# Second layer norm of a GNN kernel: last tile's product in column halves, batch statistics, final scaling shared by VectorE and ScalarE

## The reference

```python
def _L1_gnn_ref(x, edge_index, W1, b1, W2, b2):
    h = jax.nn.relu(x @ W1 + b1) @ W2 + b2
    row, col = (edge_index[0], edge_index[1])
    agg = jax.ops.segment_sum(h[col], row, num_segments=h.shape[0])
    return h + agg

def _layernorm(x, axis=-1, eps=1e-05):
    m = jnp.mean(x, axis=axis, keepdims=True)
    v = jnp.var(x, axis=axis, keepdims=True)
    return (x - m) / jnp.sqrt(v + eps)

x = _layernorm(x + _L1_gnn_ref(x, edge_index, W1, b1, W2, b2), axis=-1)
```

## Time and profile before

| what | value |
|---|---|
| runs | 252.47, 253.5, 253.42 us, median 253.42 |
| the profiled execution's own time | 252.69 us |
| its span | 250.7 us |
| TensorE's granted clock, mean | 0.974 |
| busy: TensorE, VectorE, ScalarE, GpSimd | 92%, 62%, 53%, 35% of the span |
| last matmul ends | about 245.03 us |
| last store issued, landed | 248.0, about 250.25 us |

### The profile page before, as it was taken

How to read it: one execution, slowest core, us unless ns; L and a number is a source line. 1 busy time by engine, 2 the same in 40 slices (tenths; PEclk the granted TensorE clock), 3 DMA queues, 4 the chain that set the end, 5 groups by cost and what they waited for, 6 DMA issues and landing times.

```text
span 250.7 us, 3851 instructions
## 1 busy us (share of the span) xinstructions
PE 230.5 (92%) x1433; PEld 197.8 (79%) x1433; DVE 155.9 (62%) x366; ACT 133.3 (53%) x229; POOL 87.6 (35%) x81
## 2 busy tenths in 40 slices
PE   0837999999999999999999999999999997999990
PEld 0826997777888888888888888888889995888970
DVE  1679799873966344555554326164695997786274
ACT  0636674753858057445445505356552549915373
POOL 5510000003920006565654500424277459501241
PEclk9975999999999999999999999999999999999997
DMA  4478600000066601111000097504019900000334
GB/s 111 144 243 229 147 3 0 4 0 5 0 247 241 205 1 44 42 42 42 3 0 0 2 204 143 105 3 88 18 35 165 222 32 0 3 0 1 128 126 158
DMA packets 32322, 19.96 MB, mean 80 GB/s; under 512 B 21927, under 2 KB 27084, under 8 KB 32302
## 3 DMA queue, kind: packets, MB, share of 16 engines
q1 hardware_dynamic: 31796, 19.45, 29.2%
q0 software_dynamic: 160, 0.13, 0.2%
q10 hardware_dynamic: 346, 0.10, 0.2%
HBM read 8.51 MB, written 5.92 MB: 58 GB/s over the span
## 4 chain that ended last, share of the span: by engine, by line
PE 77%; DVE 10%; DMA 5%; POOL 3%; ACT 2%; issue 1%; SPq 0%; DVEq 0%; POOLq 0%; ACTq 0%
PE ps L1282 22%; PE ps L1265 22%; PE ps L1209 17%; PE ps L1328 8%; PE ps L1346 6%; DVE hot_s L844 2%; PE ps L1189 2%; DMA src_i<-in_src 2%; DMA pairs<-pair 2%; DMA run<-pairs,start_i 1%; PE ps L1160 1%; DVE hot_k L847 1%; DVE xl L819 1%; DVE ln_s L1036 1%; POOL ul L526 1%
## 5 line engine op out<-in xcount | busy, mean ns | idle before, releaser
L940 DVE BATCH_NORM_STATS2 small_t<-ps 128x6 f32<-128x500 f32 (+1 forms) x36 | 21.6, 600 | 38.7 <-PE ps L1265 25.2
L1209 PE MATMUL ps<-AT,xh 128*128 128x500 f32 (+2 forms) x120 | 43.3, 371 | 0.0
L1209 PE MATMUL ps<-AT,xl 128*128 128x500 f32 (+2 forms) x120 | 41.5, 356 | 0.0
L1265 PE MATMUL ps<-h0h,wh 128*128 128x500 f32 (+1 forms) x96 | 33.9, 353 | 0.0
L1265 PE MATMUL ps<-h0h,wl 128*128 128x500 f32 (+1 forms) x96 | 33.9, 353 | 0.0
L1265 PE MATMUL ps<-h0l,wh 128*128 128x500 f32 (+1 forms) x96 | 33.8, 352 | 0.0
L476 POOL TENSOR_TENSOR wl<-w1s,wh 128x512 fp32r<-128x512 f32 x8 | 10.1, 1302 | 47.3 <-ACT AT L565 47.3
L481 POOL TENSOR_TENSOR wl<-w2s,wh 128x512 fp32r<-128x512 f32 x8 | 11.1, 1382 | 43.9 <-ACT wh L680 43.9
L1209 PEld LDWEIGHTS ps<-AT,xl 128*128 128x128 f32 (+1 forms) x120 | 23.2, 193 | 2.7
L1209 PEld LDWEIGHTS ps<-AT,xh 128*128 128x128 f32 (+1 forms) x120 | 23.1, 193 | 2.7
L565 ACT ACTIVATE AT<-ps 128x500 fp32r<-128x500 f32 x25 | 14.8, 590 | 17.8 <-PE ps L1189 17.6
(11 more groups left out here) (144 smaller groups left out, 503.8 us busy)
## 6 DMA issues: line engine op xcount, KB each, us to landing
turns<-half_out SPq DMA_DIRECT2D x10, 320.0 KB, 2.2
out<-x SPq DMA_DIRECT2D x9, 256.0 KB
w1s<-in_L_gnn_W SPq DMA_DIRECT2D x4, 512.0 KB, 6.1
w2s<-in_L_gnn_W SPq DMA_DIRECT2D x8, 256.0 KB, 2.7
xs<-in_x SPq DMA_DIRECT2D x1, 1280.0 KB, 7.9
xs<-in_x SPq DMA_DIRECT2D x1, 1024.0 KB
lws<-in_L_gnn_W SPq DMA_DIRECT2D x1, 512.0 KB, 5.1
lw2s<-in_L_gnn_W SPq DMA_DIRECT2D x1, 512.0 KB, 4.2
```

The costliest lines, as they stand in the source:

```text
L940: link(nc.vector.bn_stats(stats[:, 6 * c:6 * c + 6], ps[:, zbank(t, c), 0:c1 - c0]))
L1209: last = mm(o, part[0:r, k, d * P:d * P + P], AT[0:r, k, c0:c1], start=(k == 0 and j == 0), stop=(k == NT - 1 and j == 1))
L1265: last = mm(ps[:, zbank(t, c), 0:c1 - c0], w[:, t, d * P:d * P + P], h[c][:, d, :], start=(d == 0 and j == 0), stop=(d == DT - 1 and j == 2))
```

## The change

The last tile (`LAST` = 9) gets a path of its own, and the other nine are scaled by GpSimd.

- TensorE: tile 9's product is computed in two halves of 256 columns, six matmuls each. The halves go to different banks (the second to the bank of tile 5), and each raises `y_sum`.
- VectorE: `ln2_half(h)` adds a half to `x1` (no row sum) and takes its statistics (`bn_stats`); `ln2_last` combines them (`bn_aggr`), then scales tile 8's columns, and then makes tile 9's two columns and scales columns 0 to 255.
- ScalarE: for tile 9 only the root, straight from the variance, and the scaling of columns 256 to 511.
- GpSimd: scales tile 8 too.
- SyncE: stores tiles 0 to 7, then tile 9, then tile 8.

The diff, without the names of two new semaphores:

```diff
@@ -325,7 +325,13 @@
 
         XP_A = CH[1][1] // P
 
-        pool_tiles, dve_tiles = list(range(0, NT - 2)), list(range(NT - 2, NT))
+        LAST = NT - 1
+        pool_tiles = list(range(LAST))
+        YH = [(0, D // 2), (D // 2, D)]
+
+        def y_half(h):
+            b = y_banks[(LAST + h) % len(y_banks)]
+            return ps[0:rows[LAST], b, YH[h][0]:YH[h][1]]
 
 
 
@@ -424,9 +430,12 @@
                 turn_back(k)
             sp.wait_ge(z_sum, BT)
             sp.dma_start(lw2s[:, :, :], lw2.rearrange("(k p) n -> p k n", p=P)).then_inc(lw2_in, 16)
-            for k in range(NT):
-                by, tiles = (out_pool, pool_tiles) if k in pool_tiles else (out_dve, dve_tiles)
-                sp.wait_ge(by, tiles.index(k) + 1)
+            for k in pool_tiles[:-1] + [LAST, pool_tiles[-1]]:
+                if k == LAST:
+                    sp.wait_ge(out_dve, 1)
+                    sp.wait_ge(out_act, 1)
+                else:
+                    sp.wait_ge(out_pool, k + 1)
                 sp.dma_start(out[P * k:P * k + rows[k], :], x1[0:rows[k], k, :]).then_inc(stored, 16)
             sp.wait_ge(stored, 16 * NT)
             sp.wait_ge(src_in, 16)
@@ -777,10 +786,18 @@
                                      bias=epsc[0:r, :], scale=1.0 / D ** 3).then_inc(ln2_std, 1)
 
             v_high(0)
-            for s in range(NT):
+            for s in range(LAST):
                 if s in v_before:
                     v_high(v_before[s])
                 ln2_root(s)
+
+            r = rows[LAST]
+            act.wait_ge(ln2_var_last, 1)
+            nc.scalar.activation(ln_std[0:r, LAST:NT], ln_mv[0:r, LAST, 1:2], ACT.Sqrt, bias=epsc[0:r, :]
+                                 ).then_inc(ln2_std, 1)
+            act.wait_ge(ln2_aff, NT)
+            nc.scalar.activation(x1[0:r, LAST, YH[1][0]:YH[1][1]], x1[0:r, LAST, YH[1][0]:YH[1][1]], ACT.Identity,
+                                 bias=ln_r[0:r, LAST, 1:2], scale=ln_r[0:r, LAST, 0:1]).then_inc(out_act, 1)
 
 
         @block.vector
@@ -1120,10 +1137,25 @@
                 nc.vector.tensor_scalar(ln_r[0:r, k, 1:2], ln_m[0:r, k:k + 1], ln_r[0:r, k, 0:1], -1.0 / D,
                                         ALU.mult, ALU.mult).then_inc(ln2_aff, 1)
 
-            def ln2_apply(k):
-                r = rows[k]
-                v.wait_ge(ln2_aff, k + 1)
-                nc.vector.tensor_scalar(x1[0:r, k, :], x1[0:r, k, :], ln_r[0:r, k, 0:1], ln_r[0:r, k, 1:2],
+            def ln2_half(h):
+                r = rows[LAST]
+                x1_half = x1[0:r, LAST, YH[h][0]:YH[h][1]]
+                v.wait_ge(y_sum, NT + h)
+                v.wait_ge(base_set, NT)
+                link(nc.vector.tensor_tensor(x1_half, y_half(h), x1_half, ALU.add))
+                link(nc.vector.bn_stats(ln_s[0:r, LAST, 6 * h:6 * h + 6], x1_half))
+
+            def ln2_last():
+                r = rows[LAST]
+                nc.vector.bn_aggr(ln_mv[0:r, LAST, :], ln_s[0:r, LAST, 0:12]).then_inc(ln2_var_last, 1)
+                ln2_scale(LAST - 1)
+                v.wait_ge(ln2_std, NT)
+                link(nc.vector.reciprocal(ln_r[0:r, LAST, 0:1], ln_std[0:r, LAST:NT]))
+                nc.vector.scalar_tensor_tensor(out=ln_r[0:r, LAST, 1:2], in0=ln_mv[0:r, LAST, 0:1], scalar=-1.0,
+                                               in1=ln_r[0:r, LAST, 0:1], op0=ALU.mult, op1=ALU.mult).then_inc(ln2_aff, 1)
+                v.wait_ge(ln2_aff, NT)
+                x1_half = x1[0:r, LAST, YH[0][0]:YH[0][1]]
+                nc.vector.tensor_scalar(x1_half, x1_half, ln_r[0:r, LAST, 0:1], ln_r[0:r, LAST, 1:2],
                                         ALU.mult, ALU.add).then_inc(out_dve, 1)
 
             v.wait_ge(b2_in, 16)
@@ -1131,15 +1163,15 @@
             for k in range(NT):
                 base(k)
             v_low(0)
-            for s in range(NT + 1):
+            for s in range(LAST):
                 if s in v_before:
                     v_low(v_before[s])
-                if s < NT:
-                    ln2_sum(s)
+                ln2_sum(s)
                 if s >= 1:
                     ln2_scale(s - 1)
-                    if s - 1 in dve_tiles:
-                        ln2_apply(s - 1)
+            for h in range(2):
+                ln2_half(h)
+            ln2_last()
 
         @block.tensor
         def _(pe):
@@ -1340,12 +1372,16 @@
                     pe.wait_ge(x1_last_set, NT)
                 if k >= len(y_banks):
                     pe.wait_ge(ln2_sum_set, k - len(y_banks) + 1)
-                for m in range(LT):
-                    f = m * N + P * k
-                    for j, (part, w) in enumerate(((vh, lw2h), (vl, lw2h), (vh, lw2l))):
-                        last = mm(ps[0:r, y_banks[k % len(y_banks)], :], part[:, f:f + r], w[:, m, :],
-                                  start=(m == 0 and j == 0), stop=(m == LT - 1 and j == 2))
-                last.then_inc(y_sum, 1)
+                if k == LAST:
+                    pe.wait_ge(ln2_sum_set, k - len(y_banks) + 2)
+                for o, (c0, c1) in ((y_half(0), YH[0]), (y_half(1), YH[1])) if k == LAST else (
+                        (ps[0:r, y_banks[k % len(y_banks)], :], (0, D)),):
+                    for m in range(LT):
+                        f = m * N + P * k
+                        for j, (part, w) in enumerate(((vh, lw2h), (vl, lw2h), (vh, lw2l))):
+                            last = mm(o, part[:, f:f + r], w[:, m, c0:c1], start=(m == 0 and j == 0),
+                                      stop=(m == LT - 1 and j == 2))
+                    last.then_inc(y_sum, 1)
 
             pe.wait_ge(xpl_set, DT - 2)
             pe.wait_ge(xpl_mid, 1)
```

More of the change, by code:

```diff
@@ L261, in gnn_kernel @@
         v_sum, vh_set, vl_set, base_set = sem("v_sum"), sem("vh_set"), sem("vl_set"), sem("base_set")
-        y_sum, ln2_sum_set, ln2_var, ln2_std, ln2_aff, out_pool, out_dve = (
-            sem(n) for n in ("y_sum", "ln2_sum_set", "ln2_var", "ln2_std", "ln2_aff", "out_pool", "out_dve"))
+        y_sum, ln2_sum_set, ln2_var, ln2_std, ln2_aff, out_pool, out_dve, out_act, ln2_var_last = (
+            sem(n) for n in ("y_sum", "ln2_sum_set", "ln2_var", "ln2_std", "ln2_aff", "out_pool", "out_dve", "out_act", "ln2_var_last"))
         full = P * (N // P)
```

## The result

| | before | changed |
|---|---|---|
| median of 20 runs each, us | 252.93 (251.9 to 253.5) | 254.0 (253.04 to 254.75) |
| ratio, 95% interval | | 1.0045 [1.0032, 1.0058] |
| profiled execution: its time, its span | 252.69, 250.7 | 253.77, 251.9 |

A forecast was written before the change was run, and what follows sets the result against it. The prediction took the last tile's chain, hopping between engines after TensorE's product to the last store's landing, as the bound. Later issue +0.20 and second store +0.40 made +0.60 on 253.42: 254.0 us, range 252.8 to 255.0.

The forecast's parts named there:

- The product in halves: Last tile on TensorE: twelve small matmuls end at 245.07, 0.04 us later than six large; the added wait costs nothing.
- The sums: Last tile's statistics on VectorE: only 0.3 of 0.9 us is hidden under TensorE; the root starts 0.17 us later.
- Columns: Last tile's scaling columns on VectorE after the root: reciprocal 0.16 us to 247.30, then a product ending at 247.49.
- The 98 x 1 product: VectorE's product of two SBUF columns for the last tile: 0.16 us, not held by GpSimd's scaling of tile 8.
- Rival B: Last tile's two-column product held until GpSimd finishes tile 8: everything behind 0.5 us later, +1.1 us, 254.5; chance 0.13.
- VectorE's half: Last tile's scaling of 256 columns on VectorE: 0.41 us alone, held by GpSimd's tile 8, ending about 248.16.
- The last scaling: Last tile scaled in halves: ScalarE's takes 0.61 us to 248.13, VectorE's ends level; store issued at 248.20, +0.20 us.
- The stores: SyncE's last two stores: tile 8's queues behind the last tile's, 0.40 us of the landing's +0.60.
- The sum: Whole change: 0.20 us later issue plus 0.40 for the second store, +0.60 us, giving 254.0 us.
- Rival A: Last two stores overlap and the chain is at its short bound: +0.0 to +0.3 us, 253.4 to 253.7; chance 0.22.
- Rival C: Both last stores drain at the last store's 183 GB/s: +1.6 us, 255.0; chance 0.12.
- Rival D: Last tile's chain: VectorE's instructions overlap more than counted, -0.2 us, 253.2; chance 0.03.

The follow-up runs named there:

- e8: Changed kernel with last tile's product whole, its offset column by tensor_scalar, stores in tile order: tail (tile 8's sum to span end) 7.44 us, ratio 1.0022.
- e1: Changed kernel with the last tile's offset column made by tensor_scalar instead of a product of two SBUF columns: tail 7.77 us against 8.19, ratio 1.0066.
- e7: Changed kernel with GpSimd's operation on tile 8 replaced by a maximum with immediate 0, tile 8's norm left out: tail 7.98 us, 253.1 us (one run).
- e4: Kernel before with only the last two stores swapped, tile 9's ahead of tile 8's: tail 7.67 us against 7.02, ratio 1.003.
- e6: Changed kernel with GpSimd making columns of tiles 7 and 8, VectorE scaling the last tile whole, stores in tile order: tail 7.37 us, ratio 1.0012.

## Why the prediction was right or wrong, point by point

**The product in halves: right.** The forecast end was 245.07, the measured one 245.09; TensorE's added wait cost nothing.

**The sums: right.** First add 244.65 (forecast 244.75), second 245.56 (245.65), combination 0.21 (0.22), root from 246.72 (246.81). It held that the halves would win nothing (the root starts 0.05 later in the tail, forecast 0.17), and e8 shows it from the other side.

**Columns: wrong.** "The 98 x 1 product (0.16)" took 0.59, held by GpSimd until 247.83. The forecast had weighed the rule of the Trainium skill (SBUF — State Buffer, "SBUF: two separate sides") against one row, and went by the row. Rival B, at 0.13, was the true course, and its sum, +1.1 us and 254.5, is the nearest to the tail's +1.17. Its price of 0.5 for the hold was somewhat high (0.38 at the issue and 0.42 of tail by e1), its price for the stores, the forecast's 0.40, too low. The row was too weak for the weight put on it: it stood beside a different GpSimd operation (a maximum with an immediate, not a scaling with column operands), and e7 shows that such an operation doesn't hold the product to its end. The forecast saw that GpSimd's operation would meet the tail of the chain, but took VectorE's half for the victim; the product comes first, waits GpSimd out, and leaves the half untouched.

**The last scaling: right for ScalarE**, 0.60 against 0.61. **For VectorE's half wrong**: the forecast said clearly more than 0.41, and it took 0.41, since the product had already waited GpSimd out. In e1, without that, it was held 0.07 us.

**The stores: mechanism right, size short.** The forecast was +0.40 for tile 8's store behind the last one, of which the queue was the larger part; the change showed 0.65 of surplus behind the issue, and e4 priced the swap alone at 0.65. The bulk of the data was not late: it ended at 250.7, 2.15 us after the last tile's issue, where the forecast had 2.3. Two issues in a row are 0.40 us apart from start to start (248.55 and 248.95), not 0.36, which mattered little beside that. What was short is the end: the forecast put tile 8's landing 0.35 us behind its bulk, while here late packets ran on for another 0.45 us and the landing came at about 251.4, 0.7 behind the bulk. The two stores overlapped in part: 215 GB/s over the first 0.6 us is 0.13 MB of the last tile's 0.20, so the rest moved beside tile 8's rows, at 387 together. The Trainium skill (DMA: Bandwidth & Descriptors, "Queues, rings and completion order") has each DMA engine consume its ring in order; no row here tells the two tiles' packets apart, so that isn't shown.

**The sum.** The forecast was +0.20 of later issue and +0.40 of stores, +0.60 together; measured were +0.52 and +0.65, +1.17 in the tail and 1.0045 in the runs. The later issue is the statistics' 0.05, the product's 0.38 over the 0.21 that the like column product took before, and about 0.1 of ScalarE's slower scaling and the issue behind it. The time given, 254.0, is what was measured, but by luck: it was reckoned from the median of three runs, 253.42, and the median of twenty is 252.93. Half a microsecond too much in the base made up for half a microsecond too little in the change, and that half is for the most part a hold that the forecast had put at nothing. The call of no change beyond 0.5% held by a little, with the interval reaching to 0.58%.

Rival A (the second store nearly free by overlap) fell with e4, 0.65 us for the swap alone. Rival C (both stores drain at 183 GB/s) fell with the traffic: 0.46 MB from 249.3 to 251.15 are 250 GB/s, above C's bound of 215. Rival D's gain never came.

## What to carry to other kernels

Where an instruction of one engine can be held by another engine's, price it beside the long one that it will meet, not by a row from elsewhere: here a one-element product cost 0.38 us more as a product of two SBUF columns than as a scaling by a column operand (0.42 in the tail), and the cheap form computes the same. The last stores belong in the order in which their data are ready; a finished tile of 256 KB kept behind the last one cost 0.65 us at the end. And before cutting a last tile in two, to overlap its sums with its product, look whether the engine behind is idle when the first piece is ready; here it was busy with an earlier tile's columns, and the cut was worth 0.04 us; where it was freed 0.23 us sooner (e6), the statistics were done 0.22 us sooner.

## What the runs showed of the hardware

- A VectorE operation on a single element per partition was held like a wide one when it had two SBUF tensors: 0.59 us instead of 0.16 beside a GpSimd scaling with column operands, to the end of that scaling. The same product with one tensor and a column operand was not held (0.21). The Trainium skill (SBUF — State Buffer, "SBUF: two separate sides") has a VectorE operation with two SBUF inputs wait for a GpSimd operation that reads SBUF, and the trace agrees, down to one element.
- The hold is not always for the whole of GpSimd's instruction: beside a maximum with an immediate, 1.53 us long, the product took 0.42 and ended 0.9 us before GpSimd. There the measurement differs from the page's "for the whole instruction".
- GpSimd's maximum with an immediate took 1.53 us for 128 x 512, its multiply and add with two column operands 0.77.
- A scaling of 512 columns on VectorE with two column operands, started 0.21 us into a GpSimd scaling, took 0.84 instead of 0.55, and ended 0.28 after it.
- The last tile's rows, 98 of 2 KB, left at 183 to 249 GB/s, first or second in the order of the stores; a tile of 128 rows at 328 to 379.
- The tail of one kernel repeats from one profiled execution to the next within the rounding of the span (8.19 and 8.20; 7.77 and 7.77), while whole runs scatter over more than 1.5 us.
